# Attention: rows of ones filled by VectorE, most of GpSimd's constants set behind its first normalisation, waits for constants placed where they are read

## What is computed

```python
x = L0_attn_x                                  # (16, 512, 256)
xn = _layernorm(x, axis=-1)
x = x + _L0_attn_ref(xn, ...) + _L0_ffn_ref(xn, ...)

# _L0_ffn_ref: causal attention of 16 heads, then a mixture of 7 experts (2 per row) and a shared one
x = x + mla(rmsnorm(x, w_ln1), ...)
x = x + moe(rmsnorm(x, w_ln2), ...)

# mla, the part that matters here
kk = jnp.concatenate([k, k_rope], axis=-1)
qq = jnp.concatenate([q, q_rope], axis=-1)
scores = jnp.einsum('bqhd,bkhd->bhqk', qq, kk) * scale
scores = jnp.where(causal[None, None], scores, jnp.finfo(scores.dtype).min)
probs = jax.nn.softmax(scores, axis=-1)

# _L0_attn_ref: a selective scan over 512 time steps for 16 batch rows
state = jnp.clip(state * dA + x_t[:, :, None] * dB, -10.0, 10.0)
```

## Time and profile before

| | us |
|---|---|
| median of 3 runs | 4619.2 (4618.07 to 4622.37) |
| profiled execution, device time | 4624.27 |
| its span (first to last instruction) | 4622.4 |
| TensorE busy in the span | 3818.7 (83%) |
| VectorE | 2992.2 (65%) |
| ScalarE | 2502.0 (54%) |
| GpSimd | 2258.6 (49%) |

### The profile page before, as it was taken

One profiled execution on the slowest core, in us unless ns is written; L12 is line 12 of the kernel. 1 busy time (PEld: TensorE's weight loads), 2 busy tenths in 40 slices (PEclk: granted clock), 3 DMA queues, 4 the chain that ended last, 5 costly groups with the idle time before them and its releaser, 6 DMA issues.

```text
span 4622.4 us, 72113 instructions
## 1 busy us (share of the span) xinstructions
PE 3818.7 (83%) x22840; PEld 2878.8 (62%) x22840; DVE 2992.2 (65%) x5611; ACT 2502.0 (54%) x6473; POOL 2258.6 (49%) x1253
## 2 busy tenths in 40 slices
PE   4888888888888857999588888888888888888886
PEld 2444444444444436777477777777777777777776
DVE  3445454554555322222398888888988888988987
ACT  1433434443434422333477776777768677776774
POOL 4233233333323220000377776767777677777774
PEclk8889999998998878999798999999899998999998
DMA  2322223322322216666222221222222222222221
GB/s 84 95 74 82 92 79 94 95 86 75 96 80 75 73 44 206 206 210 204 77 83 72 74 84 67 81 77 82 72 77 83 75 74 81 74 78 74 81 77 39
DMA packets 268587, 419.76 MB, mean 91 GB/s; under 512 B 60245, under 2 KB 232662, under 8 KB 245656
## 3 DMA queue, kind: packets, MB, share of 16 engines
q1 hardware_dynamic: 255896, 380.98, 25.5%
q0 software_dynamic: 12288, 33.57, 2.1%
HBM read 330.56 MB, written 83.10 MB: 89 GB/s over the span
## 4 chain that ended last, share of the span: by engine, by line
PE 14%; POOL 12%; ACT 9%; DVE 9%; issue 7%; DMA 1%; DVEq 0%; SPq 0%; ACTq 0%; POOLq 0%
POOL m_ub L1532 10%; ACT m_dA L1650 6%; PE m_Y L1900 6%; PE m_Y L1910 3%; DVE m_PR L1754 2%; DVE m_PR L1762 2%; DVE m_S L1754 2%; DVE m_S L1762 2%; POOL m_yg L1542 1%; PE m_Y L1913 1%; PE m_F L1873 1%; PE m_F L1854 1%; DVE m_ub L1739 1%; PE m_F L1865 1%; POOL m_dtx L1511 1%
## 5 line engine op out<-in xcount | busy, mean ns | idle before, releaser
L1532 POOL TENSOR_TENSOR m_ub<-m_Bb,m_dtx 128x2048 f32<-128x2048 f32 x256 | 1156.8, 4543 | 503.9 <-PE m_Y L1900 497.5
L1650 ACT ACTIVATE m_dA<-m_dt,m_a_neg 128x128 f32<-128x128 f32 x4096 | 1210.0, 389 | 27.2 <-DVE m_S L1762 23.2
L1900 PE MATMUL m_Y<-m_ub,m_ident 128*128 128x128 f32 x8192 | 1029.7, 291 | 207.7 <-DVE m_ub L1739 205.3
L1900 PEld LDWEIGHTS m_Y<-m_ub,m_ident 128*128 128x128 f32 x8192 | 1010.6, 206 | 217.4 <-DVE m_ub L1739 213.6
L534 ACT ACTIVATE f_pt<-f_X 128x512 f32<-128x512 f32 (+1 forms) x704 | 371.5, 554 | 720.6 <-PE f_X L822 690.2
L609 DVE TENSOR_REDUCE f_nm<-f_Y 128x1 f32<-128x512 f32 (+3 forms) x896 | 433.3, 530 | 361.9 <-PE f_Y L816 357.9
L1754 DVE SCALAR_TENSOR_TENSOR m_PR<-m_dA,m_S 128x512 f32<-128x512 f32 x512 | 355.8, 695 | 213.5 <-ACT m_dA L1650 84.4
L815 PE MATMUL f_Y<-f_kst,f_qst 96*128 96x512 bf16 (+3 forms) x1024 | 283.4, 332 | 109.3 <-DVE f_nm L609 92.0
L1754 DVE SCALAR_TENSOR_TENSOR m_S<-m_dA,m_PR 128x512 f32<-128x512 f32 x512 | 354.8, 693 | 12.0
L1762 DVE CUSTOM_DVE_ANT_1 m_PR<-m_PR,m_ub 128x512 f32<-128x512 f32 x512 | 353.0, 689 | 0.2 <-DVE m_PR L1754 0.2
L1762 DVE CUSTOM_DVE_ANT_1 m_S<-m_S,m_ub 128x512 f32<-128x512 f32 x512 | 353.0, 689 | 0.0
(11 more groups left out here) (241 smaller groups left out, 6644.2 us busy)
## 6 DMA issues: line engine op xcount, KB each, us to landing
m_Bb<-m_bc_dram SPq DMA_DIRECT2D x64, 1024.0 KB, 4.7
m_Cb<-m_bc_dram SPq DMA_DIRECT2D x64, 1024.0 KB, 4.7
f_parts_dram<-f_parts SPq DMA_DIRECT2D x32, 768.0 KB, 4.5
f_kst<-f_parts_dram SPq DMA_DIRECT2D x192, 128.0 KB, 2.6
f_qst<-f_parts_dram SPq DMA_DIRECT2D x192, 128.0 KB, 2.6
e_rows<-sorted_rows SPq DMA_DIRECT2D x70, 256.0 KB, 2.7
e_wg<-Wg SPq DMA_DIRECT2D x70, 256.0 KB, 2.9
e_wu<-Wu SPq DMA_DIRECT2D x70, 256.0 KB, 3.9
```

The lines of the kernel that those rows point to most:

```text
L1532: pool.tensor_tensor(ub[:, h, i, :, :], Bb[:, s, :, :], dtx[:, par, m, None, s * SN:(s + 1) * SN].to_broadcast([P, NST, SN]), ALU.mult).th ...
L1650: last = act.activation(dA[:, h, i, n, :], dtt[:, par, m, s * SN:(s + 1) * SN], ACT.Exp, scale=a_neg[:, m, n:n + 1])
L1900: last = pe.matmul(Y[:, i * SN:(i + 1) * SN], ident[:, :], ub[:, h, i, n, :], start=False, stop=(n == NST - 1), skip_group_check=True)
```

## The change

Three things are done to the constants of `build_attn`.

1. The rows of ones of `kst[0]` and `kst[1]` are filled by VectorE, as its first two instructions, and count on `q_scaled`. The product that reads the scaled query weights waits for `q_scaled` at 3 in place of 1.
2. GpSimd fills `ident` and the four columns of `consts` first. The 20 other constants stand in `masks_and_ones`, which it runs behind its last small operation of step `h1` of batch element 0.
3. VectorE has no wait for constants at its start; it waits for all 26 in step `rank` of element 0. TensorE waits for 6 at its start, and for all 26 in front of `s1` of element 0.

```diff
+        for q, value in enumerate((-0.5, 0.5, 1e-5, -1.0)):
+            fixed(pool.memset(consts[:, q, :], value))
+
+        def masks_and_ones():
+            fixed(pool.memset(identb[:, :], 0.0))
...
+            fixed(pool.memset(va[:, :, :, HD:HD + 1], 1.0))
+            fixed(pool.memset(va[:, :, :, HD + 1:VA], 0.0))
...
-        for p in range(2):
-            fixed(pool.memset(kst[p][KS:KS + PARTS, :, :], 1.0))
...
                 tt(sc1[:, 10, :], sc1[:, 8, :], sc1[:, 7, :], ALU.mult).then_inc(sc_step, 1)
+                if isinstance(b, int) and b == 0:
+                    masks_and_ones()
...
-    N_CONST = 28
+    N_CONST, N_CONST_FIRST = 26, 6
...
     def _(dve):
-        dve.wait_ge(const_ready, N_CONST)
+        for p in range(2):
+            dve.memset(kst[p][KS:KS + PARTS, :, :], 1.0).then_inc(q_scaled, 1)
...
             if kind == "rank":
+                if isinstance(b, int) and b == 0:
+                    dve.wait_ge(const_ready, N_CONST)
...
         pe.wait_ge(w_loaded, W_ALL)
-        pe.wait_ge(const_ready, N_CONST)
+        pe.wait_ge(const_ready, N_CONST_FIRST)
...
-                    pe.wait_ge(q_scaled, 1)
+                    pe.wait_ge(q_scaled, 3)
...
             if kind == "s1":
+                if isinstance(b, int) and b == 0:
+                    pe.wait_ge(const_ready, N_CONST)
```

More of the change, by code:

```diff
@@ L424, in _ @@
                                  base=0, pattern=[[-1, P]], channel_multiplier=1))
[L425 to L449, removed]
@@ L450, in _ @@
-        fixed(pool.memset(va[:, :, :, HD:HD + 1], 1.0))
-        fixed(pool.memset(va[:, :, :, HD + 1:VA], 0.0))
-        for p in range(2):
-            fixed(pool.memset(kst[p][KS:KS + PARTS, :, :], 1.0))
+        for q, value in enumerate((-0.5, 0.5, 1e-5, -1.0)):
+            fixed(pool.memset(consts[:, q, :], value))
+        def masks_and_ones():
+            fixed(pool.memset(identb[:, :], 0.0))
+            fixed(pool.affine_select(out=identb[:, :], in_=identb[:, :], compare_op=ALU.not_equal, fill=1.0,
+                                     base=0, pattern=[[-1, P]], channel_multiplier=1))
+            fixed(pool.memset(mask_q[:, :], 0.0))
+            fixed(pool.affine_select(out=mask_q[:, :], in_=mask_q[:, :], compare_op=ALU.is_ge, fill=MASKED,
+                                     base=0, pattern=[[-1, P]], channel_multiplier=1))
+            fixed(pool.memset(mask_k[:, :], 0.0))
+            fixed(pool.affine_select(out=mask_k[:, :], in_=mask_k[:, :], compare_op=ALU.is_ge, fill=MASKED,
+                                     base=0, pattern=[[1, P]], channel_multiplier=-1))
+            fixed(pool.memset(before[:, :, :], 0.0))
+            fixed(pool.affine_select(out=before[:, :, :], in_=before[:, :, :], compare_op=ALU.is_ge, fill=1.0,
+                                     base=0, pattern=[[-1, ER], [1, ER]], channel_multiplier=0))
+            fixed(pool.memset(onesb[:, :], 1.0))
+            fixed(pool.memset(tri[:, :], 0.0))
+            fixed(pool.affine_select(out=tri[:, :], in_=tri[:, :], compare_op=ALU.is_ge, fill=1.0,
+                                     base=0, pattern=[[-1, P]], channel_multiplier=1))
+            for e in range(ER):
+                fixed(pool.memset(run_[:, e:e + 1], float(e * REGION)))
+            fixed(pool.memset(va[:, :, :, HD:HD + 1], 1.0))
+            fixed(pool.memset(va[:, :, :, HD + 1:VA], 0.0))
```

## The result

The kernel measured 4589.4 us in the median of 12 runs (4563.5 to 4602.0), the one before 4618.6 in 12 runs taken beside it. The ratio is **0.9945, with a 95% interval of 0.9918 to 0.9972**: faster by 0.55%, and clear of no change. The forecast was 4615.1 us, with a range that ended at 4607.0. One disturbed run of the kernel before, 5142.9 us, is left out of the ratio.

A forecast was written before the change was run, and what follows sets the result against it. No engine was full; a chain of waits behind GpSimd's constant fills bounded the start. Statistics 4.1 us earlier, with the other parts costing nothing, gave 4619.2 - 4.1 = 4615.1 us, range 4607 to 4621.

The forecast's parts named there:

- The front: Start of element 0, from the fills to the normalised rows: every step 4.1 to 4.2 us earlier.
- The price: VectorE's two fills of ones at its start: 8.64 us each as an upper reading, 17.1 us taken for both.
- The weights and the waits: VectorE's scaling waiting for loaded weights, and the new waits on TensorE and VectorE: all met in time, costing nothing.
- The quick fill: Front of VectorE's stream: fills at half price or less, weights then set the start, 12.1 us earlier, 4607.1 us; chance 0.10.
- The slow fill: Front of VectorE's stream: two cycles an element, fills end at 35.1 us, 12.9 us later, kernel 4632.1 us; chance 0.04.
- The step that failed: From the start chain to the kernel's end: a start 4.1 us earlier ends the kernel 4.1 us earlier.
- The clock rival: TensorE's first projections: clock rising at the same instant gives 4617.1 us (0.13, with a lost start), rising at once 4611.2 (0.09).
- The measure of noise: Whole kernel: a measurement tells about 0.2%, or 9.2 us, from no change; the runs shown spread over 4.3 us.

The follow-up runs named there:

- the two places tried: The kernel before with the wait in all 24 score steps (ratio 0.9990), or with 44 repeated waits, 22 instructions, at TensorE's start (0.9976).
- 11 ahead: The kernel before with 22 repeated waits, making 11 more instructions, at TensorE's start: median 4604.9 us, ratio 0.9995.
- 44 ahead: The kernel before with 44 more instructions at TensorE's start: median 4607.2 us, ratio 0.9996.
- its twin with one wait: The change with TensorE's wait for all constants before the first score step only; against the kernel before, ratios 0.9993 and 0.9975, medians 4610.2 and 4605.8 us.
- the third run of the change: The unaltered change, timed a third time against the kernel before: median 4587.5 us, ratio 0.9949.

## Why the prediction was wrong

**The front: right up to the first projection.** The fills begin at 0.88 us (0.92 forecast) and take 17.08 (17.1); the statistics start at 17.96 (18.0). The price was scaled by elements from two fills of 512 words into PSUM, by the distance of their starts; the rows' own durations would have given 15.4 us, and the new rows, 6.88 us each, are short of the distance in the same way. Seven small steps later the normalised rows are 4.21 us earlier (4.1 to 4.2). GpSimd's moved constants ended at 30.33 (30.6), far ahead of its next addition. The weights and the waits cost nothing. Behind the first projection the forecast no longer holds: the mask product was to come 4.1 us earlier and came 6.34. The quick fill, given a chance of 0.10, is not what VectorE does: 8.54 us for 8192 elements is one element in 1.04 ns. The slow fill is out as well.

**The step that failed** is "All later work of the block hangs on this chain through semaphores, and the two later blocks begin when it has ended", with the sum that followed from it: so many microseconds earlier at the start, so many at the end. It has two holes. The change was read as one more wait on TensorE, in front of "the first s1". The diff doesn't restrict it to the first; the wait stands in all 24 score steps, and 22 instructions were added ahead of two loops that were never looked at. I priced the wait, which was nothing, and not the instruction. And what code does later was taken to be independent of what stands ahead of it. The runs showed in its place: 22 instructions on TensorE, in either of the two places tried, bring a stall of 0.5 to 1.9 us into the odd chunks of the scan and a block of 2397 to 2415 us (six traces with the stall), against 2418 to 2425 with none or 11 ahead (four traces). The means are 2408.5 and 2422.3, a difference of 14 us; the trace with 44 ahead, 2408.5 with no stall, stands apart from both; counted with those that have no stall it would make the difference 11. The timings of the change against its twin with one wait give 13 ± 6.5 for the 22 instructions. With the 4.2 us of the start that makes 17 to 18, and the three timings of the change give 18.7, known to some 10 us. That the sum comes out so near is in part luck: the part ahead of the scan alone varies by 22 us between traces of the change.

**The clock rival** looked at the right resource, and for the smaller part. It priced the first 12 us of TensorE's work at -3.9 to +2.0 us, and there it came true in part: against the trace before, the first score product came 6.3 us earlier in the trace after, 2.1 more than the front's 4.2, but in the third run of the change 2.8 us earlier (67.8 against 70.5), 1.4 less. With either front its start moves by over 3 us from trace to trace. What mattered more were 13 passes of a loop 2200 us later, where the length of a wait of 2.5 to 5 us in front of a burst goes with its clock. The hint was on the page of before, in a group that was not read: the product with the output weights had 110.2 us of idle time and took 481 ns, against 384 with no low clock.

**The measure of noise** was too small. "What a measurement of this kernel can tell from no change is about 0.2%" was taken as 9.2 us, and the three runs at hand, within 4.3 us, as its spread. The 35 runs of the kernel before on one chip reach over 58.7 us. The medians of the kernel before are 4618.6, 4609.5, 4609.4 and 4615.5 us in the four sets of runs, so a range of 14 us in width was narrow even without the missed effect; but no noise of this size explains a median of 4589.4.

## What to carry to other kernels

A wait that is long met costs no time where it stands, but it can be an instruction, and in a stream with loops it moves all code behind it; count a change's instructions on every engine, and look at the "issue" idle time of the loops behind and at the packets of the instruction queue. Where a burst of matrix products follows a wait of 3 to 5 us, look at the mean time of its first products; some unread products in the idle time gave 1.25% here (the kernel before, 58.5 us), over ten times the 4.2 us by which the start was moved. When a gain shows in a block that the change doesn't touch, undo the one thing that moved its code before believing the theory that led to the change.

## What the runs showed of the hardware

- **A stall can pay.** TensorE stands still for 1.37 us and a chunk gets 2.5 us shorter (71.8 against 74.3), as the product behind runs 8 in 1.97 and not in 3.75 us.
- **The stall goes with fetching the loop's code.** The profile puts it down to "issue", and it comes and goes with the number of instructions ahead: 1.9, 8.7 and 16.4 us in all for 0, 11 and 22, and 0 for 44, where no packet of the instruction queue starts between the first and the last end of the loop on TensorE. In what way a packet holds TensorE up isn't shown. In the kernel before and most others the queue moves 232 packets in 3.80 MB, 16.4 KB each:

```profile
q8 instruction: 232, 3.80, 0.3%
```

In the odd chunks, where TensorE goes back to the loop's start at about 49 us, the trace of before has packets of that queue at about 48, 50, 53 and 58 us of the chunk, in the even ones only one in that stretch. The Trainium skill, "Runtime: NRT & Kernel Launch", section "Instruction fetch mechanics", says that instructions come in blocks of 16 KiB and that a taken branch out of what is held forces a fetch; the size of the packets and their crowding behind the jump agree with that, while its word that crossing a block is mostly hidden fits only the kernels with hardly a stall.

- **VectorE's fills cost by the element:** 8.54 us for 8192 of bf16, 4.28 for 4096 words with the same bytes; and the row of a long fill shows 6.88 and 3.47 us, a fifth less than the time from one to the next.
- **One program, one chip, 58.7 us of spread** in 35 runs. Two traces of the change, on two chips, differ by 12.8 us in the scan (2409.9 and 2397.1), with 7 and 4 slow odd chunks, and three by 22 us in the part ahead of it (2172.8 to 2195.2).
